# Where VectorE computes the attention denominators, the quotients and the layer norm roots in a fused graph kernel

## What is computed

```python
e = leaky(a_src[src] + a_dst[dst]); p = exp(e - segment_max(e)[dst])        # gnn: edge softmax, 4 heads
out = segment_sum(p / denom[dst] * h_src[src], dst)                          # then layer norm, prelu
Q, K = elu(xn @ Wq) + 1, elu(xn @ Wk) + 1                                     # mix: linear attention, 8 heads
Z = 1 / (Q . K.sum + eps);  msg = (Q . KV) * Z @ Wm;  msg = layernorm(msg, g1, b1)
msg = layernorm(relu(concat(xn, msg) @ W1) @ W2, g2, b2)
x = x + gnn + (xn + msg)
x = x + ffn(layernorm(x))                                                     # ffn: 8 experts of 3 layers, routed
```

## The kernel before

| piece | engine, line | stands in batch |
|---|---|---|
| denominators' products, 16 rows | TensorE L1427 | 3, behind the batch's second half |
| `denominators`: add eps, reciprocal | VectorE L1000, L1003 | 4, between the second and third sum |
| numerators, halves 0 and 1 | TensorE L1439 | 4 and 5; half 0 waits for L1000, half 1 for the first quotient |
| `quotients`, halves 0 and 1 | VectorE L1009 | 5 and 6, between the second and third sum |
| `attended` transposes | TensorE L1448, ScalarE L1220 | 6; wait for both quotients |
| `merge`, and the copy of it | TensorE L1458, ScalarE L1224 | 7 and 8 |
| `statistics` | VectorE L1018 | 8, 9 (this chunk), 3, 10 (chunk before) |
| `deviations`: 8 aggregates L1032, 12 dependent small operations L164 to L170, L1036; joint for both layer norms | VectorE | 10, between the second and third sum |
| `normalize` | ScalarE L1232 | 10 (this chunk), 14 (chunk before); waits for L1036 |
| `m_turned` transposes | TensorE L1469, ScalarE L1238 | 11; wait for `normalize` |
| `hidden` | TensorE L1480, ScalarE L1243 | 12 to 15 |

## Time and profile before

### The profile page before, as it was taken

One profiled execution on the slowest core, in us unless ns is written; L12 is line 12 of the kernel. 1 busy time (PEld: TensorE's weight loads), 2 busy tenths in 40 slices (PEclk: granted clock), 3 DMA queues, 4 the chain that ended last, 5 costly groups with the idle time before them and its releaser, 6 DMA issues. The chain is left out here.

```text
span 5071.8 us, 85791 instructions
## 1 busy us (share of the span) xinstructions
PE 4346.8 (86%) x23103; PEld 3430.5 (68%) x23104; DVE 3826.5 (75%) x9797; ACT 2279.7 (45%) x4346; POOL 1844.4 (36%) x1702
## 2 busy tenths in 40 slices
PE   8964888888788877878778888599999999999999
PEld 7853555555555655555555555378888888888888
DVE  8864777777777777778777777787788777877786
ACT  5531333333333333333333333266666666666666
POOL 2135666666666666666656656000000000000000
PEclk9986888888888888889888888799999999999999
DMA  5544656666556666566666566310000000000000
GB/s 184 171 134 121 174 173 180 181 173 181 171 172 179 180 182 172 169 175 181 185 173 177 171 172 171 118 41 26 25 13 25 25 25 13 25 25 25 13 25 17
DMA packets 440044, 601.74 MB, mean 119 GB/s; under 512 B 41544, under 2 KB 366672, under 8 KB 439888
## 3 DMA queue, kind: packets, MB, share of 16 engines
q1 hardware_dynamic: 360016, 378.46, 22.9%
q0 software_dynamic: 79872, 221.62, 17.7%
HBM read 312.66 MB, written 287.25 MB: 118 GB/s over the span
## 5 line engine op out<-in xcount | busy, mean ns | idle before, releaser
L855 POOL DMA_INDIRECT acc<-h_tab,strips x1664 | 1780.4, 1070 | 1073.7 <-issue 496.4
L989 DVE SCALAR_TENSOR_TENSOR acc<-acc,strips,ps 128x260 f32<-128x260 f32 x1664 | 793.2, 477 | 636.2 <-PE ps L1355 288.4
L1355 PE MATMUL ps<-acc 128*128 128x260 f32 x3328 | 1082.6, 455 | 42.3 <-DVE acc L989 32.9
L1355 PEld LDWEIGHTS ps<-acc 128*128 128x128 f32 x3328 | 657.8, 220 | 155.7 <-DVE acc L989 50.6
L974 DVE TENSOR_TENSOR acc<-acc 128x512 f32<-128x512 f32 x832 | 563.9, 682 | 0.0
L1858 ACT ACTIVATE exp<-ps,bn 128x512 f32<-128x512 f32 (+1 forms) x400 | 310.0, 775 | 491.6 <-PE ps L1925 491.0
L1172 ACT ACTIVATE strips<-ps 128x512 bf16<-128x512 bf16 x416 | 247.9, 596 | 602.8 <-remote 317.1
L1923 PE MATMUL ps<-w_hi,b_hi 128*128 128x256 f32 x1568 | 444.8, 284 | 1.2 <-DVE exp L1762 1.2
L1925 PE MATMUL ps<-w_hi,b_lo 128*128 128x256 f32 x1568 | 443.7, 283 | 0.0
L1924 PE MATMUL ps<-w_lo,b_hi 128*128 128x256 f32 x1568 | 443.6, 283 | 0.0
L1770 DVE TENSOR_TENSOR a_lo<-exp,a_hi 128x512 fp32r<-128x512 f32 (+1 forms) x400 | 261.1, 680 | 168.7 <-ACT a_hi L1860 142.4
(11 more groups left out here) (264 smaller groups left out, 8512.3 us busy)
## 6 DMA issues: line engine op xcount, KB each, us to landing
side_tab<-acc SPq DMA_DIRECT2D x416, 520.0 KB
acc<-h_tab,strips POOLq DMA_INDIRECT x1664
acc<-xnt_tab SPq DMA_DIRECT2D x50, 512.0 KB
h_tab<-proj SPq DMA_DIRECT2D x25, 520.0 KB, 6.7
exp<-side_tab SPq DMA_DIRECT2D x100, 130.0 KB, 2.3
proj<-in_x SPq DMA_DIRECT2D x25, 512.0 KB, 5.3
base_tab<-proj SPq DMA_DIRECT2D x25, 512.0 KB, 3.3
xnt_tab<-proj SPq DMA_DIRECT2D x25, 512.0 KB, 6.0
```

The lines of the kernel that those rows point to most:

```text
L855: pool.indirect_dma_start(G[s][:, b * GU + u], None, h_tab, bass.IndirectOffsetOnAxis(REC[s][:, b * GU + u, 0:1], 0)).then_inc(g_in[s], 16)
L989: nc.vector.scalar_tensor_tensor(A[:, (b % 2) * GU + u], A[:, (k - 1) % (2 * GU) if k else 2 * GU], smt[s][:, k:k + 1], ps[u][:, 0:MW], AL ...
L1355: nc.tensor.matmul(ps[u][:, 0:MW], S32[b % 2][:, u], G[s][:, b * GU + u], start=True, stop=True).then_inc(g_mm.sem, 1)
```

## The change

On VectorE, `denominators`, both `quotients` and `deviations` leave `mix_between` and go to a new function `mix_after`, called behind the batch's fourth sum. The denominators move from batch 4 to the end of batch 3, the quotients from batches 5 and 6 to the ends of batches 4 and 5. The deviations stay in batch 10 and go to its end. No other stream is edited, and no instruction is added or taken away.

```diff
-                    if cur and i == 4:
-                        denominators(n)
-                    if cur and i in (5, 6):
-                        quotients(n, i - 5)
                     if cur and i in (8, 9):
                         statistics(n, 0, i - 8)
                     if prev and i == 10:
                         statistics(n - 1, 1, 1)
-                    if i == 10:
-                        deviations(n)
...
+                def mix_after(n, i):
+
+                    cur, prev = chunks(n)
+                    if cur and i == 3:
+                        denominators(n)
+                    if cur and i in (4, 5):
+                        quotients(n, i - 4)
+                    if i == 10:
+                        deviations(n)
...
                         if here:
                             add(g, s, b, 3)
+                            mix_after(n, s * GQ + b)
```

## The result

The changed kernel takes 5007.57 us (median of 9 runs, 4984.40 to 5011.69) against 5039.48 for the kernel before (median of 9 runs on the same chip, 5023.42 to 5064.86). The ratio is 0.9921, 95% interval 0.9902 to 0.9939: some 40 us faster, 1.6 a chunk (it goes by the means, 5042.4 and 5002.9; the medians differ by 31.9). The forecast was 85 us, 3.4 a chunk. The time lies in the wide range (4865 to 5040) and just outside the forecast's own (4905 to 5000). The sign is right, and the size is twice too large.

A forecast was written before the change was run, and what follows sets the result against it. In batches 4 to 6 TensorE and VectorE wait for each other; in 7 and 8 VectorE is the bound. Gains 2.9 + 0.5 + 0 = 3.4 us a chunk, times 25 = 85 us: 4947.5, own range 4905 to 5000, wide 4865 to 5040.

The forecast's parts named there:

- Part 1: Batches 4 to 6: earlier quotients let TensorE's second numerators go up to 2.99 us sooner; gain 2.9 us a chunk.
- the replay of the earlier trace: One chunk's batches 4 to 6 traced through the moved quotients: first sum of batch 6 2.3 us earlier, plus 0.6.
- VectorE becomes the later one: Batches 4 to 6: VectorE, no longer TensorE, sets batch 6's first sum; chunk falls to 16.05 us, VectorE share 94%.
- Part 2: Denominators at batch 3's end: the numerators' wait for them shrinks; 0.5 us a chunk taken, bounds 0 and 3.2.
- Part 3: Deviations at batch 10's end: TensorE's 4.09 us stall goes, normalize comes later; counted 0, bounds 1.40 us either way.
- one wait takes the other's place: Batches 10 to 12: the wait for normalize replaces the one-hot transposes' stall, L1469 keeping its time; counted 0.
- Rival 1: Batches 4 to 6: stalls gone, TensorE runs all at 2.4 GHz, VectorE only bound; 176 us saved, 4856; chance 0.13.
- Rival 2: Batches 3 to 6: the chunk's loads make TensorE's results late, so the stall only moves; 15 us saved, 5017; chance 0.22.
- Rival 3: Batches 10 to 12: transposes 1.40 us later, next half 0.95 slower at low clock; 59 us lost, 5091; chance 0.09.
- Rival 4: Change fails its purpose: denominators wait at batch 3's end for L1427 every time, losing 1.2 us a chunk; 4977; chance 0.03.

The follow-up runs named there:

- f2: Kernel before with denominators and quotients moved, deviations at their old place, on the slower chip: 4994.93 us, 0.9906 of the kernel before.
- e3: Kernel before with the denominators alone moved, to the end of batch 3, on the quicker chip: 4635.41 us, 1.0008.
- e1: Kernel after with the deviations put back at their old place, denominators and quotients moved, on the quicker chip: 4580.56 us against 4632.34, 0.9884.
- e4: Kernel before with the quotients alone moved, to the ends of batches 4 and 5, on the quicker chip: 4580.73 us, 0.9887.
- e2: Kernel before with the deviations alone moved, behind batch 10's fourth sum, on the quicker chip: 4662.04 us, 1.0063.
- g1: The kernel after, unchanged, run again on a quicker chip: 4602.02 us against 4631.12 for the kernel before, 0.9935.
- l1 to l4: Slower chip: loads BTU, BTQ cut to 32 columns, in kernel before 0.9993, after 0.9903; loads BX, BTQ moved to batches 7, 9, in kernel after 0.9915, before 1.0001.
- f3: Kernel after with the deviations and their statistics ahead of batch 10's first sum, on the slower chip: 4985.49 us, 0.9888 of the kernel before.
- g2: Kernel after with the deviations at the front of batch 10, on a quicker chip: 4574.86 us, 0.9874 of the kernel before.

## Why the prediction was right and wrong

**Part 1, the quotients: right in mechanism, mis-sized (2.9 us a chunk, measured 2.1).** The step that failed is the replay of the earlier trace rows. I took one chunk's stall for that of all 25, and the 2.99 us that its second numerators stood for a wait for the quotient, where the row itself said "issue". On the quicker chip, where no late results show, the waits that name the quotient are 1.4 us a chunk for the numerators (the longest 2.9) and 0.5 for the transposes, and the saving is 2.1. On the slower chip, for which the forecast was made, parts 1 and 2 together were put at 3.4 and measured 1.9 (f2; 1.3 to 2.5 by its interval). There the windows of batches 4 to 6 came out nearly as forecast and misled as much as the replay did, for batches 7 and 8 gave part of it back. That this part is the lateness of TensorE's results, met at L1000, L1009 and L933 instead, is my reading: on the quicker chip neither the late results nor the giving back appear, but no run here takes the lateness away on the slower one. That VectorE becomes the later one, at a share of about 94%, came true on the quicker chip (95%); on the slower one it is 363.98 / 488.80 = 74%.

**Part 2, the denominators: mis-sized (0.5, measured 0).** e3 has 1.0008 (0.9999 to 1.0017), and e1 equals e4. The step that failed is to credit the wait of L1439 for L1000 to the time at all: on the quicker chip it is 40.3 us in e4, is gone in e1, and the time stays. On the slower chip L1444's wait for L1000 fell from 80.5 to 35.1 us, and L1000 itself waits 49.3 us for "remote".

**Part 3, the deviations: wrong (0, measured 1.2 a chunk in e2, and 0.9 between e1 and g1).** The first half of the step held: L1336's stall goes, `normalize` becomes the late one, and in the chunks shown L1474 starts only some 0.15 us later (in e1 1554.59 - 1547.84 = 6.75 us behind L1032; in g1 1565.26 - 1559.76 = 5.50, with L1032 itself later by two sums and a one-hot matrix, 1.40 us). What failed is the sentence that one wait takes the other's place at no cost. It counted TensorE's starting times and not its clock. In the rows before, batch 11's second half ran at the low level, out of VectorE's way. In e1 the low level reached batch 12's first half in ten of 24 chunks only; with the deviations moved it is there in all 24, and VectorE waits for that half.
The Trainium skill ("TensorE: Matmul & The Clock Gate", HAM oscillation) says that an engine which idles between bursts starts each burst at the lower clock. The rows agree in part: batch 12's halves take 1.94 and 2.05 us behind the moved pause against 1.04 and 1.09, but the first transposes behind it still take 0.68, with the granted clock at 1.00 up to their start. I had weighed the rule for batches 4 to 6 and not here.

**Rival 1** (the clock comes back, 4856) didn't happen: PEclk in the windows of batches 4 to 6 rose from 0.71 to 0.76 on average and not to 1.00, and they took 20.4 us a chunk and not 16.4. **Rival 2** was half right. TensorE's results are late in all these kernels on the slower chip, and part of the stall moves, as its sentence said; but the chunk's own loads are not the cause (l1 to l4), and 47 us remain of the first two parts (f2), not 15. **Rival 3** had the clock right, 0.95 us at batch 12, and its other term wrong: the transposes start 0.15 us later and not 1.40. As a slower kernel it came about only in e2, where parts 1 and 2 are missing. **Rival 4** fell with the waits that vanished.

So the sum is 2.1 + 0 - 1.1 = 1.0 us a chunk on the quicker chip (1.1 as the mean of 1.2 and 0.9; measured 29 us, 1.2), and on the slower one 1.6, of which 1.9 belongs to the first two parts and -0.3, within the noise, to the deviations. The best version found is f3 and g2, with the deviations ahead of batch 10's sums: 0.9888 (0.9858 to 0.9918) and 0.9874 (0.9857 to 0.989). On the quicker chip it beats the kernel after by its interval (0.9935); on the slower one the intervals overlap. On neither is it told apart from the deviations at their old place (0.9906 and 0.9884).

Open: what makes TensorE's results late on the slower chips. The loads `BTU` and `BTQ` are excluded; the gathers were tried on a quicker chip only.

## What to carry to other kernels

A stall that the profile puts down to "issue" or "remote" is not yet a wait for the instruction that one means to move: price it by the waits that name that instruction, and look for the rest at the next instruction in the row. And a wait that does name it may still be off the path, as the denominators' was. When a pause of TensorE is exchanged for another, ask which matmuls stand behind each and who waits for these, since they may run at 1.2 GHz; and look at all chunks, not at one, since the low stretch does not reach equally far in each. Try the parts of such a change alone: here one gained 52 us, one nothing, and one lost 30.

## What the chip showed that was not expected

The same kernel takes 5039 us on some chips and 4632 on others. Windows of the edge stage and the expert stage, the kernel before on the first chip (the profiled execution, 5073.61 us), then e3 (1.0008 of before) on a quicker one:

```profile
448.00:3231.00 2783.00, 2244.63 (x10724) 1589.23 (x10724) 2084.75 (x5416) 921.10 (x2027) 1714.81 (x1598) 0.87 0.61 175
3231.00:5071.00 1840.00, 1778.39 (x10404) 1565.44 (x10404) 1433.00 (x3422) 1168.61 (x1762) 0.00 (x0) 0.98 0.09 26
```

```profile
409.00:2788.00 2379.00, 2100.86 (x10712) 1501.41 (x10710) 2069.75 (x5409) 915.13 (x2023) 1754.83 (x1614) 0.93 0.71 205
2788.00:4631.00 1843.00, 1781.38 (x10404) 1567.05 (x10404) 1432.25 (x3422) 1169.21 (x1762) 0.00 (x0) 0.98 0.09 26
```

The expert stage is equal within 3 us. The first stage is 39 us shorter and the edge stage 404 us: the difference lies in the stages where gathers and loads run. VectorE idles 264.1 us before L989 in e3, 237.4 of it for L1360, and 474.7 in f2 on the slower chip, 171.6 of it "remote".
